# The high and low parts of the q and k weights, interleaved column by column

## What is computed

```python
# x: 2048 tokens x 512, 32 heads of 128 for q, k and v
q, k, v = x @ wq, x @ wk, x @ wv          # f32
p = softmax(causal(q @ k.T) * SCALE)      # in sequences of 32 tokens
out = (p @ v) @ wo
x = x + out
```

## Time and profile before

| | |
|---|---|
| median of 3 runs | 2121.44 us |
| profiled execution | 2125.11 us |
| its span, first to last instruction | 2123.3 us |
| busy: PE, DVE, ACT, POOL | 2088.3, 1380.0, 718.5, 1261.8 us |
| mean granted TensorE clock | 0.999 of full speed |

### The profile page before, as it was taken

How to read it: one execution, slowest core, us unless ns; L and a number is a source line. 1 busy time by engine, 2 the same in 40 slices (tenths; PEclk the granted TensorE clock), 3 DMA queues, 4 the chain that set the end, 5 groups by cost and what they waited for, 6 DMA issues and landing times. The chain is left out here.

```text
span 2123.3 us, 36936 instructions
## 1 busy us (share of the span) xinstructions
PE 2088.3 (98%) x11914; PEld 1810.9 (85%) x11914; DVE 1380.0 (65%) x2615; ACT 718.5 (34%) x1444; POOL 1261.8 (59%) x1319
## 2 busy tenths in 40 slices
PE   7999999999999999999999999999999999999999
PEld 5888888989888898989888898989887778878887
DVE  8767777676767777665666566565656776645444
ACT  5333232332223232332323233322323744443332
POOL 3578585777757676767758576776755642133220
PEclk9999999999999999999999999999999999999999
DMA  7421213211111226211111211111112200001110
GB/s 241 154 63 46 53 47 84 54 52 47 49 52 44 63 60 206 81 41 41 40 40 40 69 49 36 43 40 40 40 62 73 96 21 0 0 1 40 40 40 20
DMA packets 123783, 122.43 MB, mean 58 GB/s; under 512 B 35905, under 2 KB 102113, under 8 KB 121793
## 3 DMA queue, kind: packets, MB, share of 16 engines
q1 hardware_dynamic: 92865, 110.01, 16.8%
q10 hardware_dynamic: 29568, 7.34, 1.6%
q0 software_dynamic: 1280, 4.20, 0.7%
HBM read 108.27 MB, written 13.28 MB: 57 GB/s over the span
## 5 line engine op out<-in xcount | busy, mean ns | idle before, releaser
L217 PE MATMUL psum<-yc,wh 128*128 128x512 f32 x904 | 360.5, 399 | 0.3 <-PEq L270 0.3
L219 PE MATMUL psum<-yc,wh 128*128 128x512 f32 x904 | 352.4, 390 | 0.0
L218 PE MATMUL psum<-yc,wh 128*128 128x512 f32 x904 | 352.2, 390 | 0.0
L217 PE MATMUL psum<-kept,yc 128*128 128x256 f32 x896 | 255.4, 285 | 6.9 <-DVE u L1421 6.2
L1472 DVE TENSOR_TENSOR resid<-psum,resid 128x512 f32<-128x512 f32 x248 | 171.2, 691 | 134.5 <-PE psum L219 128.8
L219 PE MATMUL psum<-kept,yc 128*128 128x256 f32 x896 | 251.5, 281 | 0.0
L1023 POOL TENSOR_TENSOR wh<-wh_f,wh 128x256 fp32r<-128x256 f32 x256 | 189.8, 752 | 103.7 <-ACT wh L989 101.8
L218 PE MATMUL psum<-kept,yc 128*128 128x256 f32 x896 | 251.5, 281 | 0.0
L1023 POOL TENSOR_TENSOR wh<-raw,wh 128x256 fp32r<-128x256 f32 x192 | 143.1, 745 | 98.8 <-ACT wh L989 98.8
L219 PEld LDWEIGHTS psum<-yc,wh 128*128 128x128 f32 x904 | 169.7, 188 | 35.9
L217 PEld LDWEIGHTS psum<-yc,wh 128*128 128x128 f32 x904 | 170.1, 188 | 31.5 <-issue 0.7
(11 more groups left out here) (367 smaller groups left out, 4917.2 us busy)
## 6 DMA issues: line engine op xcount, KB each, us to landing
raw<-in_attn_w SPq DMA_DIRECT2D x96, 512.0 KB, 5.1
wo_f<-in_attn_w SPq DMA_DIRECT2D x31, 512.0 KB, 4.0
hankel<-kernel_rows SPq DMA_DIRECT2D x32, 256.0 KB, 4.8
y_parts<-stage ACTq DMA_DIRECT2D x56, 128.0 KB, 2.3
yc<-y_parts SPq DMA_DIRECT2D x7, 1024.0 KB, 5.3
resid<-in_xT SPq DMA_DIRECT2D x4, 1024.0 KB, 10.0
outT<-wide SPq DMA_DIRECT2D x16, 256.0 KB, 2.6
kept_f<-in_l_w SPq DMA_DIRECT2D x3, 1024.0 KB, 5.3
```

The source lines that it names most:

```text
L217: pe.matmul(out, w[0], x[0], start=start, stop=False)
L218: pe.matmul(out, w[0], x[1], start=False, stop=False)
L219: return pe.matmul(out, w[1], x[0], start=False, stop=stop)
```

## The change

In `wh`, a slot used to hold 256 high columns and then 256 low ones. Now it holds pairs: high and low of column 0, high and low of column 1, and so on. Every access to a part of `wh` then has a step of two elements, 8 bytes. V's weights, `wo` and the activations are as before.

```diff
     def __init__(self, stack, sb, sem, overlaid, kept_raw, kept):
-        self.wh_raw, self.wh = overlaid(stack, "wh", [P, 8, 2, 2 * DH])
+        self.wh_raw, self.wh = overlaid(stack, "wh", [P, 8, 2 * DH, 2])
...
         slot = j + (1 if j == 6 and kind in ("H1", "H3") else 0)
-        return (self.wh_raw if plain else self.wh)[:, slot, low, :]
+        return (self.wh_raw if plain else self.wh)[:, slot, :, low]
```

## The result

The changed kernel takes 2137.21 us (median of four, 2136.39 to 2140.2), the kernel before 2121.95 in the runs beside it: a ratio of 1.007 with a 95% interval from 1.0058 to 1.0081, 15.3 us slower. The forecast was no change, 2121.5 us, with chance 0.48 and a range of its own of 2117 to 2126, which doesn't hold the result; the range of 2112 to 2160 does, and "slower" had 0.35. Of the rivals the closest is (a), a price on PE for each of the 2688 matmuls with a stepped operand. Its 21.5 to 37.6 us were too much, and its first reason, a load that outlasts its cover, falls in the experiments.

A forecast was written before the change was run, and what follows sets the result against it. The prediction took PE's pace of one matmul after another in the attention loop as the bound. Load, toll and writers summed as 0 + 0 + 0 to 2121.5 us, own range 2117 to 2126, 8 in 10 within 2112 to 2160.

The forecast's parts named there:

- (a): On 2688 `wh` matmuls, load outlasts cover or toll doubles, line fetches competing with moving stream: +21.5 to 37.6 us; chance 0.23.
- its cover: On PE, the 227 ns of the 512-column matmul in flight, which hides the next weight load of at most 112 ns.
- Bound and structure: Attention loop: PE busy 1364.85 of 1370 us, its matmul pace the bound; no instruction, wait, semaphore or DMA changes.
- Step one, the load: PE's stepped weight load grows by a factor of at most 1.7 from 112 ns, stays hidden under 227 ns: cost 0.
- the ACT row: ACT reading `resid` with a step of 128 bytes, a factor of 2.1 an element; on PE this would give +21.5 us.
- Step two, the toll: The 14 ns a `wh` matmul takes over the pure 213: no change expected, bounds -37.6 to +37.6 us.
- The signs named for rival (a): On PE, steps of 0.235 to 0.241 us with `wh` and still 0.227 with `wo` beside them.
- (d): The change doesn't reach PE, loads are done as before whatever the step: 2121.5 us; chance 0.48 together with no change.
- Step three, the writers: ACT's copies and POOL's operations on `wh`: no gain, ACT up to 233 ns a copy, POOL's cost nothing or hidden under 94 ns.
- the margin of the first V weights: In each loop iteration, PE starts on V weights 0.94 us after POOL ends them; hides 94 ns more per POOL operation.
- rival (b): POOL falls behind before the first V weights, from 94 ns more an operation: +13.5 to +42 us; chance 0.12.
- Rival (c): On `wh` matmuls the toll shrinks, weights being spread over twice the lines: 2084 to 2117 us, taken as 2100; chance 0.17.

The follow-up runs named there:

- t1_trains: Kernel before with 23 unused trains of 16 PE matmuls appended after attention, stationary step varied; at 512 columns 0.230 us a step with 4 bytes, 0.233 with 8.

## Why the prediction was right and wrong

**Bound and structure** were right: PE sets the time, no wait came up, and each nanosecond on the 2688 matmuls shows. 2688 x 7.2 ns, the average growth of a step, is 19 us. With the 3.4 us of the steps beside other matmuls it is over 22, and 15 remain since the V part, where PE waited for DVE, gives some of it back.

**Step one, the load**, was right in its result, a load that stays under its cover, and the ACT row was the wrong neighbor for it: with a step of 8 bytes the load is 0.118 us for 0.112, a factor of 1.05 where up to 1.7 was allowed. The factor of 2.1 measured at 128 bytes appears from 16 bytes on (0.236 for 0.112). The Trainium skill's rule of two accesses to one 16-byte line ("Advanced Engine Details and Errata", SBUF Cachelines) fits the loads: nearly full pace at 8 bytes, 0.173 at 12, 0.236 at 16. What the prediction drew from it, a cost of 0, doesn't hold, since the cost isn't in the load. The Trainium skill's rule for VectorE's ports, full rate only on runs of two or more adjacent 4-byte words ("Vector Engine (DVE) Microarchitecture Reference", 5.2 Measured stream behaviour), doesn't carry over to PE's stationary operand, but its moving one behaves alike: with a step of 8 bytes a matmul of 512 columns takes 7.26/16 = 0.454 us, twice as long. The prediction set the listed load duration aside as the same for every load. It isn't: it went from 188 to 196 ns with 8 bytes and to 309 with 16.

**Step two, the toll**, is the step that failed. It was put at no change because `wo` and `wh` matmuls had the same pace at "unrelated addresses". They aren't unrelated: they all happened to lie well, and a shift of 64 bytes spoils them. The toll went from 14 ns over the pure 213 to about 21, not to 28; the bounds of -37.6 and +37.6 us held it, and the value inside was mis-sized: 0 where it measured +19. With plain f32, where the moving operand goes by at half the pace, neither 8 nor 16 bytes cost anything. What inside the memory makes the toll, why the step of 8 bytes costs nothing at 480 columns and fewer while a shift of 64 bytes costs the V matmuls 1.6 ns at 256, and why one layout ran at two paces, stays open; none of the runs looks into it.

**The range** held the result by luck in part. It reached up to 2160 for a load past its cover or a doubled toll, and the measured time came from neither but from a smaller growth of the toll. The signs named for rival (a) did come nearly as written, `wh` steps of 0.234 to 0.238 and `wo` steps that hardly moved (227.0 to 228.4 ns), and (d) is refuted by them. Of (a)'s second reason, line fetches that compete with the moving stream, the runs show only that the cost depends on where both operands lie.

**Step three, the writers**, was right in sign for ACT (+24 ns) and wrong for POOL, which I had as unchanged or slower. Its subtractions in place fell by 120 ns, so the margin of the first V weights grew from 0.94 to 1.73 us (858.69 + 1.49, PE at 861.91), and rival (b) had nothing to act on. I had excluded a gain for the writers since no stepped row was faster than its neighbor. Only the subtractions that read both operands from `wh` gained; those that read one from `raw` didn't (745 to 753). So the gain seems to come from where the two operands of one instruction lie, which the rows of the prediction don't vary; no run moves them alone.

**Rival (c)** was wrong in sign, though its premise is right in part: what a step takes over the pure 213 does depend on the layout, only the kernel before was already at the low end of all that were tried.

## What to carry to other kernels

On this kernel a stationary operand may be read with a step of 8 bytes with hardly a longer load, but a step of 12 bytes or more lengthens it, and a moving operand wants to be contiguous. Where fp32r matmuls of 512 columns run back to back, compare the step between starts with the 227 ns here: if it is 230 to 235, where the operands lie is a cause to try early, by moving one buffer by multiples of 16 bytes. When a buffer is resized in such a kernel, pad it to a multiple of 256 bytes, which cost nothing here, and give every layout experiment a control that only moves the buffers.

## What wasn't expected of the hardware

- 64 bytes of unused memory cost 9.8 us (2122.75 to 2132.57), 256 bytes nothing (2121.87 to 2121.93).
- The length of a stationary load isn't monotone in the step: with 256 moving columns 0.173 us at 12 bytes, 0.236 at 16, 0.241 at 32, 0.221 at 64.
- During the trains of 16 columns PE's listed time was full; the granted clock fell to its lower level, 1.2 GHz, at 1612.5 us in the second of them and came back at 1636.4 during the trains of 256 columns. Busy time and clock by stretch in t1_trains:

```profile
1612.00:1624.00 12.00, 12.00 (x57) 12.00 (x56) 0.00 (x0) 0.00 (x0) 0.00 (x0) 0.52 0.00 0
1624.00:1636.00 12.00, 12.00 (x57) 12.00 (x58) 0.00 (x0) 0.00 (x0) 0.00 (x0) 0.50 0.01 1
```

At this lower clock a load with a step of 16 bytes took (1619.93 - 1616.21)/16 = 0.233, against 0.236 at the full clock, so its length didn't follow the clock here; a contiguous one shifted by 4 bytes took (1630.62 - 1627.21)/16 = 0.213, nearly twice the 0.112 of the full clock.
- ACT's copy of 256 elements takes 408 ns contiguous, 432 with steps of 8 bytes and 664 to 676 with 16; POOL's subtraction in place 752, 632 and 678.
